# Giving GpSimd 192 instead of 128 columns of some rounds in a fused attention and MLP layer

## The reference

```
mod = silu(c) @ wmod                      # sa, ca, ga, sb, cb, gb; |ga|, |gb| at least 0.25
h   = layernorm(x) * (1 + ca) + sa
q   = h @ Wq per head                     # queries, keys and values are all q
att = softmax(4 q q^T) q                 # 16 heads, 4096 x 4096 scores each
x   = x + ga * (att @ Wp^T + bp)
h   = layernorm(x) * (1 + cb) + sb
x   = x + gb * (h + 0.5 * (silu(layernorm2(h) @ w1 + b1) @ w2 + b2))
```

## Time and profile before

| | us |
|---|---|
| median of 3 runs | 1959.11 |
| profiled execution | 1958.2 |
| its span | 1956.4 |
| PE busy / ACT busy in the span | 1868.9 / 1880.3 |
| DVE busy / POOL busy | 1490.3 / 1251.7 |

### The profile page before, as it was taken

One profiled execution on the slowest core, in us unless ns is written; L12 is line 12 of the kernel. 1 busy time (PEld: TensorE's weight loads), 2 busy tenths in 40 slices (PEclk: granted clock), 3 DMA queues, 4 the chain that ended last, 5 costly groups with the idle time before them and its releaser, 6 DMA issues.

```text
span 1956.4 us, 47545 instructions
## 1 busy us (share of the span) xinstructions
PE 1868.9 (96%) x18411; PEld 544.5 (28%) x18411; DVE 1490.3 (76%) x2543; ACT 1880.3 (96%) x1491; POOL 1251.7 (64%) x2118
## 2 busy tenths in 40 slices
PE   8788889999999999999999999999999999999999
PEld 6211112222222222222232222322232222322225
DVE  5567677778878877777887788778777778777884
ACT  6899999999999999999999999999999999999992
POOL 5173777477746776377873778467763768737770
PEclk9899999999999999999999999999999999999999
DMA  6531212122121221212112121112121121111100
GB/s 214 163 93 45 51 34 54 43 59 49 51 49 40 57 52 51 57 44 53 50 47 56 54 49 54 37 55 54 47 56 46 52 48 54 49 38 43 43 7 18
DMA packets 121391, 108.40 MB, mean 55 GB/s; under 512 B 21952, under 2 KB 120128, under 8 KB 120912
## 3 DMA queue, kind: packets, MB, share of 16 engines
q1 hardware_dynamic: 120416, 103.69, 19.8%
q10 hardware_dynamic: 752, 1.67, 0.2%
HBM read 96.49 MB, written 8.65 MB: 54 GB/s over the span
## 4 chain that ended last, share of the span: by engine, by line
ACT 50%; PE 28%; issue 12%; DVE 4%; POOL 2%; DVEq 0%; POOLq 0%
ACT attend_probs L890 29%; ACT attend_probs L896 20%; PE attend_sums L943 14%; PE attend_scores L929 8%; PE attend_out L951 3%; PE attend_scores L951 1%; ACT hidden L884 1%; PE attend_sums L957 1%; PE attend_out L957 1%; DVE attend_probs L1148 1%; DVE attend_spare L1160 1%; POOL attend_spare L858 1%; DVE attend_probs L1149 0%; DVE base L1184 0%; DVE attend_sums_sb L1114 0%
## 5 line engine op out<-in xcount | busy, mean ns | idle before, releaser
L890 ACT ACTIVATE attend_probs<-attend_scores 128x2048 f32<-128x2048 f32 x683 | 1288.3, 1886 | 8.6 <-PE attend_scores L929 8.4
L943 PE MATMUL attend_sums<-attend_probs,values 128*17 128x512 f32 x8192 | 1007.0, 597 | 2.1 <-POOL attend_probs L863 1.6
L1148 DVE COPY attend_probs<-attend_scores 128x896 f32<-128x896 f32 x578 | 630.0, 1090 | 282.8 <-PE attend_scores L929 276.1
L896 ACT ACTIVATE attend_probs<-attend_probs 128x896 f32<-128x896 f32 (+1 forms) x682 | 665.9, 976 | 5.3 <-DVE attend_probs L1148 3.1
L929 PE MATMUL attend_scores<-asks,keys 64*128 64x512 f16 x4096 | 564.5, 381 | 72.8 <-ACT attend_probs L890 66.8
L854 POOL TENSOR_TENSOR attend_spare<-attend_spare 128x256 f32<-128x256 f32 x289 | 183.0, 633 | 373.9 <-DVE attend_spare L1162 373.8
L929 PEld LDWEIGHTS attend_scores<-asks,keys 64*128 64x128 f16 x4096 | 151.2, 94 | 671.2 <-ACT attend_probs L890 543.3
L943 PEld LDWEIGHTS attend_sums<-attend_probs,values 128*17 128x17 f32 x8192 | 174.8, 96 | 507.4 <-issue 483.3
L858 POOL TENSOR_TENSOR attend_spare<-attend_spare 128x256 f32<-128x256 f32 x289 | 232.6, 805 | 24.1
L863 POOL TENSOR_TENSOR attend_probs<-attend_spare 128x256 f32<-128x256 f32 x289 | 219.4, 759 | 22.7
L861 POOL TENSOR_TENSOR attend_spare<-attend_spare,attend_probs 128x256 f32<-128x256 f32 x289 | 212.3, 735 | 24.1
(11 more groups left out here) (163 smaller groups left out, 838.7 us busy)
## 6 DMA issues: line engine op xcount, KB each, us to landing
keys<-parts_dram SPq DMA_DIRECT2D x768, 64.0 KB
keys<-parts_dram SPq DMA_DIRECT2D x256, 56.0 KB
asks<-parts_dram SPq DMA_DIRECT2D x192, 64.0 KB
start_x_in<-L_attn_x SPq DMA_DIRECT2D x8, 512.0 KB, 9.5
parts_dram<-start_q_parts SPq DMA_DIRECT2D x16, 256.0 KB, 2.6
attend_x_now<-L_attn_x SPq DMA_DIRECT2D x8, 512.0 KB, 4.1
out<-base SPq DMA_DIRECT2D x15, 256.0 KB, 2.6
asks<-parts_dram SPq DMA_DIRECT2D x64, 56.0 KB
```

What stands on the lines that cost most here:

```text
L890: act.activation(place(n, 2), ps_scores[:, 0:4, :], ACT.Exp, scale=scale).then_inc(exps_done, 1)
L896: act.activation(cols, cols, ACT.Exp, scale=scale).then_inc(exps_done, 1)
L943: last = pe.matmul(ps_sums[32 * hq:32 * hq + E1, :], values[:, j + STEPS * b, (gg % Q_GROUPS) * Q_HEADS + hq, :], place(gg * PAIRS + Q_HEA ...
L1148: dve.tensor_copy(flat(n, 0, DIRECT), bank[:, 0:DIRECT]).then_inc(copied, 1)
```

## The change

In a pair of which one round has a tanh on ACT, each of the two rounds gives 192 columns to DVE and POOL instead of 128, and ACT's L896 takes 832 instead of 896. 55 of the 56 tanh rounds lie in such a pair, each in its own, so 55 pairs are wide and 234 stay as they are. The scratch slices get room for 192 columns a round; pairs with 128 use the first 128 of each. The order of instructions and their number stay.

```diff
-SPARE = 128
-DIRECT = 2 * BANK - SPARE
+SPARE, MORE = 128, 192
...
+TANH_ROUNDS = {at + BEHIND for at in TANH_IN}
+SPARE_COLS = {at: MORE if TANH_ROUNDS & set(pair) else SPARE for pair in SPARE_PAIRS for at in pair}
...
-        spare = a.take("spare", 5 * 2 * SPARE).rearrange("p (s r n) -> p s r n", s=5, r=2)
-        spare_whole, spare_part = spare[:, 0, :, :], spare[:, 1, :, :]
+        spare = a.take("spare", 5 * 2 * MORE).rearrange("p (s r n) -> p s r n", s=5, r=2)
...
-            return by_round[:, at % rounds:at % rounds + 2, S_RING - 1, DIRECT:2 * BANK]
+            return by_round[:, at % rounds:at % rounds + 2, S_RING - 1, 2 * BANK - SPARE_COLS[at]:2 * BANK]
+
+        def spare_rows(at):
+
+            return [spare[:, i, :, 0:SPARE_COLS[at]] for i in range(5)]
...
-                square, second, bits = (spare[:, i, :, :] for i in range(2, 5))
...
                     cols = spare_of(at)
+                    spare_whole, spare_part, square, second, bits = spare_rows(at)
...
-                        cols = flat(n + 2, 0, DIRECT if at in SPARE_ROUNDS else 2 * BANK)
+                        cols = flat(n + 2, 0, 2 * BANK - SPARE_COLS.get(at, 0))
...
-                        dve.tensor_copy(flat(n, 0, DIRECT), bank[:, 0:DIRECT]).then_inc(copied, 1)
-                        dve.tensor_scalar(flat(n, DIRECT, 2 * BANK), bank[:, DIRECT:2 * BANK], exp2_scale, LOWEST,
+                        direct = 2 * BANK - SPARE_COLS[at]
+                        dve.tensor_copy(flat(n, 0, direct), bank[:, 0:direct]).then_inc(copied, 1)
+                        dve.tensor_scalar(flat(n, direct, 2 * BANK), bank[:, direct:2 * BANK], exp2_scale, LOWEST,
                                           ALU.mult, ALU.max).then_inc(spare_t, 1)
...
+                        spare_whole, spare_part = spare_rows(first)[:2]
```

## The result

The changed kernel takes 1999.8 us (median, 1999.08 to 2001.16), the kernel before 1959.33 beside it. The ratio is 1.0206, with a 95% interval of 1.0196 to 1.0215: slower by 40 us, where 36 were forecast. The profiled execution has a span of 1997.8 us, 41.4 more than before, so the trace holds all of the difference.

The account below looks back on a forecast made before the run. ACT and PE, both 96% busy, bound the kernel; POOL would need 633 us in 592.7, 40 too much, less 8, plus 3: 35 on 1958.2 gives 1993, set at 1995 us; 80% range 1964 to 2038.

Parts of the forecast that it names:

- The cause: POOL's longer chains in seven stretches with tanh pairs make PE wait, then ACT; 35 us lost, chance 0.55.
- The sizes: POOL's seven chain instructions go from 256 to 384 columns in wide pairs: 1.33 us more, ends 0.74 and 2.0.
- ACT's term: ACT's L896 loses 64 columns, 59 ns a round; over 55 tanh rounds 3.2 us saved.
- PE's loop: L890 frees banks, PE makes scores, L890 restarts: 2.59 us in plain rounds, so no ACT gain taken there.
- The gaps in the scratch rows: Gaps between the spare buffer's two rows, in pairs that keep 128 columns, were counted at nothing.
- the backlog that is "not forgiven": POOL needs 633 us in stretches of 592.7, 40 too much; narrow pairs between give back under 0.2 each.
- The step from 653.69 to 658.71: Shortest start-to-start of POOL chains found beside running rounds, 5.02 us; 106 of them need at least 532 us.
- what was taken off and given back: Off: 8 us for POOL's lead and PE's room, 1.2 a stretch; back: 3 us for unusable POOL idle gaps.
- the lead of 0.2 to 1.5 us: Time by which POOL's chain ends before PE's weighing, for pairs weighed two rounds after their first.
- The hidden case: Rival: POOL's work stays hidden if a wide pair adds under 0.80 us; 1953 to 1956, chance 0.07.
- The heavy case: Rival: all POOL time is columns, or DVE's copies come late; 2031, up to 2045, chance 0.17 beyond 2016.

Follow-up runs that it names:

- act_only: Changed kernel with POOL's chain and DVE's split back at 128 columns a round, ACT's exponential still leaving 192; 1955.39 us against 1958.89, ratio 0.9981.
- mid160: Changed kernel with 160 columns in place of 192 in the wide pairs; 1972.09 us against 1960.43, ratio 1.0058.
- six_192: Changed kernel with one product moved from POOL to DVE in every pair and DVE's split ahead of the hidden tile's finish; 1983.09 us, ratio 1.0116.
- swap_after: Changed kernel with DVE's split for POOL put ahead of the finish of a hidden tile; 1994.93 us, ratio 1.0182.
- light_between: Changed kernel with split and chain of 72 narrow pairs up to three pairs behind a wide one cut to 64 columns a round; 1978.78 us, ratio 1.0099.

## Why the prediction was right, and where not

- The cause: right. The wait of PE at L946 behind L866 (48.6 us, "tens of us" forecast), L893 idle by PE, PE and ACT at 94%, all of the loss in the seven stretches.
- The sizes: TENSOR_TENSOR 0.82 and near 1.0 us forecast, 0.855 and 1.01 to 1.04 measured; TENSOR_SCALAR 0.51, measured 0.54 to 0.64 in the mean and 0.51 in the median. The chain from start to end, 5.8 to 6.3 forecast, is 6.1 in the mean (4.7 before). The figure of the Trainium skill's GPSIMD Engine Reference (Elementwise — side-by-side cycle accounting), 4497 ns for 2048 columns, gave an estimate of 1.44 us for the chain's growth, my rows 1.33; the trace lies between the two, 1.37 us from 4.74 to 6.12 in the mean.
- ACT's term: right in sum, 3.2 forecast and 3.5 measured by act_only, but partly by luck. The tanh rounds gave 2.3 us and not 3.2, and the plain rounds, put at nothing behind PE's loop, gave 0.9.
- The gaps in the scratch rows: nothing, as forecast.
- **The step that failed**: the backlog that is "not forgiven", as one sum over a stretch. From start to end the 106 chains of the seven stretches take 568.9 us (493.2 before), less than the 592.7 there were, and POOL idles 0.62 us a chain, where 0.1 to 0.4 were forecast. The step from 653.69 to 658.71 was not the shortest either: the trace before has 4.89 (from 512.97 to 517.86), the changed kernel 4.73. What happens instead differs among the 41 wide pairs weighed two rounds on:
  - In 11, DVE's split starts only after POOL is idle (for 1.55 to 1.96 us, as before 639.93): PE's wait has held back the scores, the pair starts anew and is late by its own path; 9.0 us of the loss stand there.
  - In 25, POOL's idle time of 0.95 to 1.03 us is not free time: the split starts before the last instruction of the chain ahead is through, takes up to 0.88 us against 0.35, and ends 0.21 to 0.29 us behind that instruction. So the lateness of a chain is passed on over DVE, although POOL idles; 15.4 us stand there. What in the chain holds the split was not tried.
  - In 5 the split is done earlier and the chain follows after 0.08 to 0.56 us (5.1 us).

One of the 25:

```profile
456.65 1.05 POOL L866 TENSOR_TENSOR attend_probs<-attend_spare 128x256 f32<-128x256 f32 x1
457.05 0.88 DVE L1165 TENSOR_SCALAR attend_spare<-attend_probs 128x384 f32<-128x384 f32 x1
...
457.96 0.56 DVE L1167 SCALAR_TENSOR_TENSOR attend_spare<-attend_probs,attend_spare 128x384 f32<-128x384 f32 x1
...
458.67 0.83 POOL L857 TENSOR_TENSOR attend_spare<-attend_spare 128x384 f32<-128x384 f32 x1 [0.96 <-DVE attend_spare L1167]
```

- The total came out near (42.0 in the stretches, 35 forecast) partly by luck. The sum gave 6.5, 8.7, 0.7, 6.5, 8.7, 2.5 and 6.5 us too much for the seven stretches before what was taken off and given back, against 5.3, 8.8, 3.9, 5.3, 8.6, 4.8 and 5.2 measured. The two stretches with long POOL gaps, where it leaves least, lose 4 to 5 us all the same. The right term was there in the text, the lead of 0.2 to 1.5 us, but was spent once a stretch instead of being set against each pair's 1.6 us.
- The hidden case's break-even of 0.80 us a pair fell with it: mid160 adds about that and loses 11.7 us.
- The heavy case (DVE late with its copies) came about in small only: L899 waits 11.1 us for L1152 in all, 3.1 before. It came when DVE was given more work, in six_192.

## What to carry to other kernels

An engine at 64% busy can have no room at all: ask how long after its input each result is needed, and set the new length against that lead, pair by pair. Then look at what an engine's idle time before an instruction is made of: a late result makes idle time on the late engine itself, and so does a neighbour whose work on the next input it has held up. A total of work against a stretch's length sees none of this. Nor is the lead alone enough, as mid160 shows (4 us by the leads, 11.8 measured). Before moving work off the bounding engine, price what it can give back at most (here 3.5 us, as its neighbour's loop is as long), and where the work lands.

## What was not expected of the hardware

Beside an instruction of DVE with two inputs in SBUF, a POOL instruction took 1.14 us instead of 0.83 (swap_after), and such a DVE instruction took 1.18 instead of 0.43 elsewhere. A TENSOR_SCALAR of DVE with one input in SBUF (L1165) is held too, from 0.35 to 0.88 us in the rows at 457.05: it ends 0.22 us behind POOL's last instruction, and 0.15 behind it where it has 256 columns. Moving L1265 out of a path into the neighbour's work gave back 5 us of an expected 15 to 22. The time of POOL's TENSOR_TENSOR goes up evenly with columns: 0.40 us for 128 (light_between), 0.61 for 256, 0.83 for 384, with equal inputs; 0.46, 0.73 and 1.0 with two different ones.
